# Adding x to the aggregate inside an accumulating transfer, so that PE transposes one sum

## The chip, the cores and the metric

One core of a Trainium2 chip runs the whole kernel. The metric is the time of one execution on the device in microseconds (us), median of several runs.

## What is computed

One layer of a graph network over N = 100000 nodes of width 128 and E = 50000 edges, followed by a layer norm. Everything is float32.

```python
deg = maximum(zeros(n).at[dst].add(1.0), 1.0)
edge_weight = (deg[src] * deg[dst]) ** (-0.5)
edge_msg = relu(edge_attr @ W1e + b1e) @ W2e + b2e
agg = segment_sum((x[src] + edge_msg) * edge_weight[:, None], dst)
combined = (1.0 + gin_eps) * x + agg
h = relu(combined @ W1n + b1n) @ W2n + b2n
out = (h + x) * rsqrt(mean((h + x) ** 2) + 1.2e-7) * rms_w
y = x + out
return (y - mean(y)) / sqrt(var(y) + 1e-5)
```

The change touches the line with `combined`. Since (1 + eps) x + agg = (1 + eps) (x + agg / (1 + eps)), the factor can be moved into the weights of the edges' sums and into W1n.

## The kernel before

The kernel has three stages: it counts degrees, it runs over the edges in 98 batches of 512 and scatters weighted sums of equal destinations into a scratch tensor in HBM (`agg_scratch`, the code's `agg_d`), and it runs over the nodes. Edges are sorted by destination, so that one row is written once; a last accumulating scatter (L562) adds what crosses partitions.

The node stage follows, and it is what the change touches. Node rows are laid out so that partition p holds 781 successive rows. A block is 16 of them on all 128 partitions: 8 KB a partition, 1 MB in all. There are 49 blocks (`BLOCKS`), and each is worked in four steps (`SPB`) of 4 x 128 nodes (`TB = 4`), thus 196 steps (`STEPS`). Every engine runs a hand-written software pipeline: in `node_step(n, u)` the engine does, for step number n, work on several older step indices m = n - lag, in the order in which the lines stand. Engines are tied only by semaphores.

- SP, `node_block(B)` (L488 to L503): waits until PE is done with the slot of block B-4 and loads `ag` of block B from `agg_scratch`; loads `xn` (x) of block B; then waits for `fin_ready` and `fin_last` of block B-6 (`OUT_LAG = 6`) and stores `on` to `out`. All goes through one queue, in order. `xn` and `ag` have four slots each, `on` has two.
- ACT: rms of m = n-6 (L684), cT of n-2 (L690, copies the transposed sum out of PSUM), hn of n-3 (L695), **xe of n (L701, (1 + eps) x)**, squares of n-5 (L709); once a block the spread of the layer norm (L678).
- PE: o of n-4 (L1074, L1078: bias and W2n), **the transposes of n-1 (L1087: four of xe, L1091: four of ag, accumulated into one bank)**, W1n of n-2 (L1098).
- DVE: res of n-4 (L910, h + x), bn_stats of n-8 (L927), q of n-7 (L934, times rms_w), some operations of 16 columns a block, z of n-7 (L966), and **on of the fourth column of n-18 (L975)**, which increments `fin_last`.
- POOL: xsc of n-6 (L575, four operations), which waits for ACT's rms; on of the first three columns of n-18 (L587, three operations), which increments `fin_ready`.

Two slots of `xsc` tie POOL to DVE: xsc of m waits for z of m-2, z of m waits for xsc of m. res of m has four slots, freed by q and by the squares.

Of the kernel before, what the change touches and what calls it, by code (L numbers as in the profile page):

```python
# [47 lines left out]
def build(nc, x, src, dst, edge_attr, W1n, b1n, W2n, b2n, W1e, b1e, W2e, b2e, gin_eps, rms_w, out):  # L48
# [4 lines left out]
    ALU = mybir.AluOpType  # L53
# [4 lines left out]
    E, ED = edge_attr.shape  # L58
    RMS_EPS = 1.1920929e-07
    LN_EPS = 1e-05  # L60

# [44 lines left out]
    with ExitStack() as ctx:  # L106
# [22 lines left out]
        rms_b = sb("rms_b", [P, D])  # L129
        eps1 = sb("eps1", [P, 1])  # L130
        rms_eps = sb("rms_eps", [P, 1])
        ln_eps = sb("ln_eps", [P, 1])
# [93 lines left out]
        ag = sb("ag", [P, AR, BN, D])  # L226
        xe = sb("xe", [P, 2, TB, D])
        cT = sb("cT", [P, 2, W])
# [14 lines left out]
        spread = sb("spread", [P, 2, BN])  # L243
        neg_mean = sb("neg_mean", [P, 4, BN])
        rstd = sb("rstd", [P, 4, BN])

# [15 lines left out]
        bias_ready = sem("bias_ready")  # L262
        eps_ready = sem("eps_ready")
        iota_set = sem("iota_set")
# [15 lines left out]
        lengths_ready = sem("lengths_ready")  # L280
        dd_ready = sem("dd_ready")
        lists_ready = sem("lists_ready")

# [23 lines left out]
        xn_in = sems("xn_in", XR)  # L307
        ag_in = sems("ag_in", AR)
        out_sent = sems("out_sent", 2)
        xe_ready = sem("xe_ready")  # L310
        cT_done = sem("cT_done")
# [19 lines left out]
        fin_ready = sem("fin_ready")  # L331
        fin_last = sem("fin_last")
        sp_passed = sem("sp_passed")
        pool_passed = sem("pool_passed")
# [177 lines left out]
        def _(pool):  # L512
# [52 lines left out]


            def node_step(n, u):
                m, s = n - 6, (u - 6) % 4
                if live(m, STEPS):
                    _, xsl, _, h = place(m, u - 6)  # L570
                    pool.wait_ge(rms_ready, at(m + 1))
                    need(pool, z_ready, m - 1)
                    apart(pool, pool_passed)
                    for j in range(TB):
                        last = pool.tensor_scalar(xsc[:, s % 2, j, :], xn[:, xsl, h + j, :], rms[:, s, j:j + 1], 1.0,  # L575
                                                  ALU.mult, ALU.mult)
                    last.then_inc(xsc_ready, 1)
                m, v = n - 18, (u - 18) % ZR
                if live(m, STEPS):
                    B, o, h = m // SPB, ((u - 18) // SPB) % 2, ((u - 18) % SPB) * TB  # L580
                    if h == 0:
                        pool.wait_ge(mean_ready, at(B + 1))
                        pool.wait_ge(rstd_ready, at(B + 1))
                        need(pool, out_sent[o], B // 2 * 16)
                        apart(pool, pool_passed)
                    for j in range(TB - 1):
                        last = pool.tensor_scalar(on[:, o, h + j, :], z[:, v, j, :],  # L587
                                                  neg_mean[:, v // SPB, h + j:h + j + 1],
                                                  rstd[:, v // SPB, h + j:h + j + 1], ALU.add, ALU.mult)
                    last.then_inc(fin_ready, 1)  # L590

            run(pool, STEPS, SPB * XR, node_step, tail=18, head=2)


        @block.scalar
        def _(act):
# [66 lines left out]

            act.wait_ge(dd_ready, 2)
            run(act, BATCHES, 2, edge_step, tail=1, head=2, peel=1)
# [4 lines left out]

            act.wait_ge(eps_ready, 1)

            def node_step(n, u):
# [18 lines left out]
                if live(m, STEPS):  # L692
                    act.wait_ge(hn_done, at(m + 1))
                    need(act, o_done, m - 1)
                    act.activation(hn[:, s, :], ps[2 + s][:, :], ACT.Relu, bias=b1n_c[:, 0:1]).then_inc(hn_ready, 1)  # L695
                m, s = n, u % 2
                if live(m, STEPS):
                    B, xsl, _, h = place(m, u)
                    act.wait_ge(xn_in[xsl], at(block_loads(B, XR)))
                    need(act, cT_done, m - 1)  # L700
                    act.activation(xe[:, s, :, :], xn[:, xsl, h:h + TB, :], ACT.Copy, scale=eps1[:, 0:1]  # L701
                                   ).then_inc(xe_ready, 1)
                m, v, s = n - 5, (u - 5) % ZR, (u - 5) % 4
# [8 lines left out]

            run(act, STEPS, SPB * XR, node_step, tail=18, head=2)


        @block.vector
        def _(dve):
# [120 lines left out]
            dve.wait_ge(wts_in, 16 * WEIGHTS)  # L838
            dve.tensor_scalar(eps1[:, :], eps1[:, :], 1.0, None, ALU.add).then_inc(eps_ready, 1)
            dve.wait_ge(src_cols, 2)  # L840
# [62 lines left out]
            def node_step(n, u):  # L903
                m, s = n - 4, (u - 4) % RR
                if live(m, STEPS):
                    _, xsl, _, h = place(m, u - 4)
                    dve.wait_ge(o_done, at(m + 1))
# [49 lines left out]
                if u % SPB == 1 and live(k, BLOCKS):  # L957
                    dve.wait_ge(spread_ready, at(k + 1))
                    dve.reciprocal(rstd[:, c, :], spread[:, c % 2, :]).then_inc(rstd_ready, 1)  # L959

                m, v = n - 7, (u - 7) % ZR
                if live(m, STEPS):
                    dve.wait_ge(xsc_ready, at(m + 1))
                    dve.wait_ge(q_ready, at(m + 1))
                    need(dve, fin_ready, m - ZR + 1)
                    dve.tensor_tensor(z[:, v, :, :].rearrange("p j d -> p (j d)"), ps[7][:, :],  # L966
                                      xsc[:, v % 2, :, :].rearrange("p j d -> p (j d)"), ALU.add).then_inc(z_ready, 1)
# [14 lines left out]
        def _(pe):  # L982
# [87 lines left out]
            def node_step(n, u):  # L1070
# [54 lines left out]
```

## Time and profile before

| | us |
|---|---|
| median of 3 runs | 2165.47 (2165.39 to 2170.3) |
| the profiled execution | 2150.24 |
| its span | 2148.5 |
| node stage, first ag transpose on PE to the end of the span | 1488.9 to 2148.5 |

A time in the rows is counted from the start of the span. A group's mean is its duration; successive instructions of one engine overlap in part, so an engine's pace is read from starts. "Idle before" is the engine's idle time just before an instruction, with the releaser behind the arrow. In a windows view the columns are the length, then for each engine the busy time and the number of instructions, the granted clock of PE (1.00 is 2.4 GHz), the DMA engines' busy share and GB/s.

### The profile page before, as it was taken

The page shows a single profiled execution, that of the slowest core. Times are in us where ns is not written, and L with a number is a line of the kernel's source. Part 1 is how long each engine was busy: PE and PEld are TensorE (multiplying, and loading weights), DVE is VectorE, ACT ScalarE, POOL GpSimd, SP SyncE. Part 2 cuts the span into 40 slices and gives each one's busy share as a digit, 9 for nine tenths or more (in the row PEclk, how much of TensorE's full clock was granted, in tenths as well). Part 3 has the DMA queues.
Part 4 walks back from the last instruction along what each step waited for, and adds up shares of the span by engine and source line. Part 5 has one row for each costly group of instructions (what it writes and reads, how often), then busy time and mean ns, then how long its engine had stood idle before and what let it go on. Part 6 is the DMA issues. An engine that isn't in the chain of part 4 may idle for free. (4 is left out here: it accounts for less than half of the span.)

```text
span 2148.5 us, 43403 instructions
## 1 busy us (share of the span) xinstructions
PE 1537.2 (72%) x11484; PEld 1127.5 (52%) x11484; DVE 1290.7 (60%) x4579; ACT 1118.8 (52%) x3879; POOL 1303.8 (61%) x2171
## 2 busy tenths in 40 slices
PE   1114995666666667666666677775999999999993
PEld 0002554544545445445545566664777777777772
DVE  2003996333334334343333466662999999999997
ACT  1003982222222222222222244444999999999994
POOL 5772002555555555555555545553588888888888
PEclk8556997688787886877877899997999999999997
DMA  7793001212212112111111112114366666666662
GB/s 284 302 412 144 0 3 31 53 54 53 53 53 54 53 53 54 54 53 53 53 53 53 52 56 58 59 61 183 128 252 248 234 242 248 253 253 234 235 246 115
DMA packets 83038, 275.63 MB, mean 128 GB/s; under 512 B 19110, under 2 KB 46300, under 8 KB 58396
## 3 DMA queue, kind: packets, MB, share of 16 engines
q1 hardware_dynamic: 57422, 231.16, 29.2%
q0 software_dynamic: 25136, 43.60, 6.9%
q14 instruction: 50, 0.41, 0.1%
q8 instruction: 16, 0.26, 0.1%
q10 hardware_dynamic: 414, 0.20, 0.0%
HBM read 154.37 MB, written 128.22 MB: 132 GB/s over the span
## 5 line engine op out<-in xcount | busy, mean ns | idle before, releaser
L542 POOL DMA_INDIRECT agg_scratch<-scaled,sca_i x390 | 387.6, 994 | 576.6 <-ACT scaled L661 484.2
L1022 PE MATMUL bank<-digits,picks 128*128 128x128 f16 x5488 | 441.1, 241 | 211.7 <-DVE picks L772 121.0
L1022 PEld LDWEIGHTS bank<-digits,picks 128*128 128x128 f16 x5488 | 382.6, 110 | 319.3 <-issue 165.3
L535 POOL DMA_INDIRECT xs<-in_x,src_x x391 | 377.5, 965 | 132.4 <-issue 118.8
L886 DVE TENSOR_TENSOR msg<-bank,xs 128x512 f32<-128x512 f32 x98 | 67.8, 692 | 549.7 <-issue 536.2
L575 POOL TENSOR_SCALAR xsc<-xn,rms 128x128 f32<-128x128 f32 x784 | 277.9, 370 | 128.9 <-ACT rms L684 125.5
L655 ACT ACTIVATE he<-bank,b1e_c 128x512 f32<-128x512 f32 x98 | 67.5, 689 | 512.7 <-remote 433.3
L587 POOL TENSOR_SCALAR on<-z,neg_mean,rstd 128x128 f32<-128x128 f32 x588 | 257.2, 445 | 0.0
L1000 PE MATMUL bank<-oh_hi,steps 128*128 128x512 f16 x392 | 143.6, 406 | 144.1 <-issue 125.8
L1049 PE MATMUL bank<-w2e,he 128*128 128x128 f32 x784 | 163.2, 374 | 111.9 <-ACT he L655 111.9
L1078 PEld LDWEIGHTS bank<-w2n,hn 128*128 128x128 f32 x1568 | 205.8, 191 | 70.2 <-issue 64.6
L772 DVE TENSOR_SCALAR picks<-highq,high_no 128x512 f16<-128x512 f16 x686 | 238.5, 361 | 0.0
L1098 PE MATMUL bank<-cT,w1n 128*128 128x512 f32 x392 | 220.7, 645 | 18.9 <-ACT cT L690 3.9
L709 ACT ACTIVATE squares<-res 128x128 f32<-128x128 f32 x784 | 232.4, 304 | 0.0
L759 DVE TENSOR_SCALAR oh_hi<-iota_h,dst_hi 128x782 f16<-128x782 f16 x392 | 132.8, 423 | 157.1 <-issue 100.6
L1049 PEld LDWEIGHTS bank<-w2e,he 128*128 128x128 f32 x784 | 142.1, 270 | 160.9 <-ACT he L655 159.8
L628 ACT ACTIVATE steps<-iota_h,dst_step 128x128 f16<-128x128 f16 x392 | 125.7, 392 | 163.3 <-issue 101.4
L1078 PE MATMUL bank<-w2n,hn 128*128 128x128 f32 x1568 | 206.7, 275 | 0.2 <-ACT hn L695 0.2
L641 ACT ACTIVATE eaT<-bank 64x512 f32<-64x512 f32 x98 | 58.0, 592 | 256.3 <-PE bank L1034 213.2
L927 DVE BATCH_NORM_STATS2 stats<-z 128x6 f32<-128x128 f32 x784 | 169.0, 278 | 0.0
L709 ACT ACTIVATION_READ_ACCUMULATOR squares<-res 128x1 f32 x784 | 154.4, 197 | 0.0
L864 DVE SCALAR_TENSOR_TENSOR sums<-sums,cont,bank 128x128 f32<-128x128 f32 x391 | 133.4, 341 | 33.5 <-issue 19.6
(145 smaller groups left out, 2601.2 us busy)
## 6 DMA issues: line engine op xcount, KB each, us to landing
agg_scratch<-zeros SPq DMA_DIRECT2D x48, 1024.0 KB
xn<-in_x SPq DMA_DIRECT2D x48, 1024.0 KB
ag<-agg_scratch SPq DMA_DIRECT2D x48, 1024.0 KB, 6.8
out<-on SPq DMA_DIRECT2D x48, 1024.0 KB, 4.9
highq<-src_high_scratch SPq DMA_DIRECT2D x98, 128.0 KB
ea<-in_edge_attr SPq DMA_DIRECT2D x97, 127.0 KB
xs<-in_x,src_x POOLq DMA_INDIRECT x391
agg_scratch<-scaled,sca_i POOLq DMA_INDIRECT x390
```

The costliest lines, as they stand in the source:

```text
L535: pool.indirect_dma_start(out=xs[:, b % XS, j, :], out_offset=None, in_=x, in_offset=bass.IndirectOffsetOnAxis(ap=src_x[:, t:t + 1], axis= ...
L542: pool.indirect_dma_start(out=agg_rows, out_offset=bass.IndirectOffsetOnAxis(ap=sca_i[:, t:t + 1], axis=0), in_=scaled[:, b % 2, j, :], in ...
L575: last = pool.tensor_scalar(xsc[:, s % 2, j, :], xn[:, xsl, h + j, :], rms[:, s, j:j + 1], 1.0, ALU.mult, ALU.mult)
L587: last = pool.tensor_scalar(on[:, o, h + j, :], z[:, v, j, :], neg_mean[:, v // SPB, h + j:h + j + 1], rstd[:, v // SPB, h + j:h + j + 1], ...
L709: last = act.activation(squares[:, s, j, :], res[:, s, j, :], ACT.Square, accum_out=ssq[:, v // SPB, s * TB + j:s * TB + j + 1])
L772: return dve.tensor_scalar(picks[:, s, c, :], highq[:, q, :], high_no[:, c:c + 1], None, ALU.is_equal)
L927: last = dve.bn_stats(stats[:, (v // SPB) % 2, (v % SPB) * TB + j, :], z[:, v, j, :])
L1000: pe.matmul(ps[0][:, :], steps[:, s, j, :], oh_hi[:, s, j, 0:512], start=first, stop=end)
L1022: last = pe.matmul(ps[s][:, j * P:(j + 1) * P], picks[:, s, c, j * P:(j + 1) * P], digits[:, d, c * P:(c + 1) * P], start=c + d == 0, stop ...
L1049: last = pe.matmul(ps[4 + s][:, j * P:(j + 1) * P], he[:, s, j * P:(j + 1) * P], w2e[:, :], start=False, stop=j == TB - 1)
L1078: last = pe.matmul(ps[4 + s][:, j * P:(j + 1) * P], hn[:, s, j * P:(j + 1) * P], w2n[:, :], start=False, stop=j == TB - 1)
L1098: pe.matmul(ps[2 + s][:, :], w1n[:, :], cT[:, s, :], start=True, stop=True).then_inc(hn_done, 1)
```

## The change

- POOL gets `add_block(B, a)`: wait until `ag` of block B has landed, then issue a transfer that adds x of the same block onto it in SBUF (`accum_op=add`). It stands at the head of POOL's step n = 4B - 4 (block 0 ahead of the loop, block 1 in step 0).
- PE waits for that transfer (`sum_in`) and transposes only `ag`: four transposes a step in place of eight. ACT's xe and its buffer are gone.
- eps: DVE works out 1 + eps, bounded away from zero, multiplies W1n by it and the run sums' factors `dd` and `fin_dd` by its inverse, ahead of the edge loop; ACT's edge loop waits for that (`dd_scaled`).
- on of the fourth column moves from DVE (n-18) to the end of ACT's step, at n-20, as scale times z plus `offset`; DVE works out `offset` = neg_mean * rstd once a block.

```diff
@@ gpsimd
+            def add_block(B, a):
+                if isinstance(B, int) and B == BLOCKS - 1:
+                    pool.wait_ge(ag_in[a], block_loads(B, AR))
+                    pool.dma_start(ag[:, a, 0:LASTC, :], x_main[:, B * BN:NPP, :], accum_op=ALU.add
+                                   ).then_inc(sum_in[a], 16)
+                    pool.dma_start(ag[0:NREM, a, LASTC, :], x[NPP * P:N, :], accum_op=ALU.add).then_inc(sum_in[a], 16)
+                else:
+                    pool.wait_ge(ag_in[a], at(block_loads(B, AR)))
+                    pool.dma_start(ag[:, a, :, :], x_main[:, bass.ds(at(B * BN), BN), :], accum_op=ALU.add
+                                   ).then_inc(sum_in[a], 16)
+
+            add_block(0, 0)
+
             def node_step(n, u):
+                B = n // SPB + 1
+                if u % SPB == 0 and live(B, BLOCKS):
+                    add_block(B, (u // SPB + 1) % AR)
                 m, s = n - 6, (u - 6) % 4
@@ scalar
-            act.wait_ge(dd_ready, 2)
+            act.wait_ge(dd_scaled, 1)
...
-                m, s = n, u % 2
-                if live(m, STEPS):
-                    B, xsl, _, h = place(m, u)
-                    act.wait_ge(xn_in[xsl], at(block_loads(B, XR)))
-                    need(act, cT_done, m - 1)
-                    act.activation(xe[:, s, :, :], xn[:, xsl, h:h + TB, :], ACT.Copy, scale=eps1[:, 0:1]
-                                   ).then_inc(xe_ready, 1)
...
+                m, v = n - 20, (u - 20) % ZR
+                if live(m, STEPS):
+                    B, o, h = m // SPB, ((u - 20) // SPB) % 2, ((u - 20) % SPB) * TB + TB - 1
+                    act.wait_ge(offset_ready, at(B + 1))
+                    if h < TB:
+                        need(act, out_sent[o], B // 2 * 16)
+                    act.activation(on[:, o, h, :], z[:, v, TB - 1, :], ACT.Identity, bias=offset[:, v // SPB, h:h + 1],
+                                   scale=rstd[:, v // SPB, h:h + 1]).then_inc(fin_last, 1)
@@ vector
-            dve.tensor_scalar(eps1[:, :], eps1[:, :], 1.0, None, ALU.add).then_inc(eps_ready, 1)
+            link(dve.tensor_scalar(eps1[:, :], eps1[:, :], 1.0, None, ALU.add))
+            dve.tensor_scalar(eps_sign[:, :], eps1[:, :], 0.0, 2.0, ALU.is_ge, ALU.mult)
+            link(dve.scalar_tensor_tensor(eps_abs[:, :], eps1[:, :], -1.0, eps1[:, :], ALU.mult, ALU.max))
+            link(dve.tensor_scalar(eps_abs[:, :], eps_abs[:, :], EPS_FLOOR, None, ALU.max))
+            link(dve.scalar_tensor_tensor(eps1[:, :], eps_sign[:, :], -1.0, eps_abs[:, :], ALU.add, ALU.mult))
+            dve.tensor_scalar(w1n[:, :], w1n[:, :], eps1[:, 0:1], None, ALU.mult)
+            link(dve.reciprocal(eps_inv[:, :], eps1[:, :]))
+            dve.wait_ge(dd_ready, 2)
+            dve.tensor_scalar(dd[:, :], dd[:, :], eps_inv[:, 0:1], None, ALU.mult)
+            dve.tensor_scalar(fin_dd[:, :], fin_dd[:, :], eps_inv[:, 0:1], None, ALU.mult).then_inc(dd_scaled, 1)
...
+                k, c = (n - 18) // SPB, ((u - 18) // SPB) % 4
+                if u % SPB == 2 and live(k, BLOCKS):
+                    dve.wait_ge(rstd_ready, at(k + 1))
+                    dve.tensor_tensor(offset[:, c, :], neg_mean[:, c, :], rstd[:, c, :], ALU.mult
+                                      ).then_inc(offset_ready, 1)
...
-                m, v = n - 18, (u - 18) % ZR
-                if live(m, STEPS):
-                    B, o, h = m // SPB, ((u - 18) // SPB) % 2, ((u - 18) % SPB) * TB + TB - 1
-                    dve.wait_ge(rstd_ready, at(B + 1))
-                    if h < TB:
-                        need(dve, out_sent[o], B // 2 * 16)
-                    dve.tensor_scalar(on[:, o, h, :], z[:, v, TB - 1, :], neg_mean[:, v // SPB, h:h + 1],
-                                      rstd[:, v // SPB, h:h + 1], ALU.add, ALU.mult).then_inc(fin_last, 1)
@@ tensor
-                    pe.wait_ge(xe_ready, at(m + 1))
+                    pe.wait_ge(sum_in[asl], at(block_loads(B, AR)))
                     need(pe, cT_ready, m - 1)
                     for j in range(TB):
-                        pe.matmul(ps[s][:, j * P:(j + 1) * P], xe[:, s, j, :], ident[:, :], is_transpose=True,
-                                  start=j == 0, stop=False)
-                    pe.wait_ge(ag_in[asl], at(block_loads(B, AR)))
-                    for j in range(TB):
                         last = pe.matmul(ps[s][:, j * P:(j + 1) * P], ag[:, asl, h + j, :], ident[:, :],
-                                         is_transpose=True, start=False, stop=j == TB - 1)
+                                         is_transpose=True, start=j == 0, stop=j == TB - 1)
```

## Rows read from the trace of the kernel before

**Rows 1.** The page: busy digits of 40 slices of the span, two engines.

```profile
ACT  1003982222222222222222244444999999999994
POOL 5772002555555555555555545553588888888888
```

**Rows 2.** Windows: the steady part of the node stage.

```profile
1552.40:2103.70 551.30, 533.93 (x3268) 390.49 (x3267) 537.88 (x1720) 544.75 (x2108) 467.65 (x1204) 1.00 0.64 241
```

**Rows 3.** Timeline of POOL, steps 21 and 193: start, us, instructions.

```profile
1549.46 1.41 POOL L575 TENSOR_SCALAR xsc<-xn,rms 128x128 f32<-128x128 f32 x4 [0.46 <-ACT rms L684]
1550.85 1.30 POOL L587 TENSOR_SCALAR on<-z,neg_mean,rstd 128x128 f32<-128x128 f32 x3
...
2101.04 1.41 POOL L575 TENSOR_SCALAR xsc<-xn,rms 128x128 f32<-128x128 f32 x4 [0.43 <-ACT rms L684]
```

**Rows 4.** Timeline of all engines, ACT's and one POOL row shown.

```profile
1802.37 0.29 ACT L684 ACTIVATE rms<-ssq,rms_eps 128x4 f32<-128x4 f32 x1
...
1802.89 1.45 POOL L575 TENSOR_SCALAR xsc<-xn,rms 128x128 f32<-128x128 f32 x4 [0.51 <-ACT rms L684]
...
1803.61 0.72 ACT L701 ACTIVATE xe<-xn,eps 128x512 f32<-128x512 f32 x1
...
1804.22 0.31 ACT L709 ACTIVATE squares<-res 128x128 f32<-128x128 f32 x1
```

**Rows 5.** Timeline of DVE, one step.

```profile
1805.04 0.69 DVE L966 TENSOR_TENSOR z<-bank,xsc 128x512 f32<-128x512 f32 x1 [0.19 <-DVE bank L934]
1805.65 0.34 DVE L975 TENSOR_SCALAR on<-z,neg_mean,rstd 128x128 f32<-128x128 f32 x1
1805.90 0.68 DVE L910 TENSOR_TENSOR res<-bank,xn 128x512 f32<-128x512 f32 x1
```

**Rows 6.** Timeline of PE, an early step: four transposes of each.

```profile
1496.71 0.60 PE L1087 MATMUL bank<-ident,xe 128*128 128x128 f32 x4
1497.14 0.60 PE L1091 MATMUL bank<-ident,ag 128*128 128x128 f32 x4
```

**Rows 7.** Timeline of SP's queue.

```profile
1552.43 0.34 SPq L503 DMA_DIRECT2D out<-on  x1
...
1783.55 0.36 SPq L503 DMA_DIRECT2D out<-on  x1
1784.16 0.33 SPq L481 DMA_DIRECT2D ag<-agg_scratch  x1
```

**Rows 8.** Waits of SP's queue, then ag's time to landing, both 1700 to 2000.

```profile
SPq L349 <- DVE on L975: 238.3, 23, 10.6
...
DMA to landing us min/median/max: 6.3/6.8/7.1
```

**Rows 9.** Timeline of POOL: scatters, and the one that accumulates.

```profile
1477.41 0.98 POOL L542 DMA_INDIRECT agg_scratch<-scaled,sca_i  x1 [0.30 <-issue]
1480.48 1.60 POOL L562 DMA_INDIRECT agg_scratch<-scaled,fin_i  x1 [2.09 <-issue]
```

**Rows 10.** DMA queues: 1700 to 2000, then 1481 to 1484: packets, MB, share.

```profile
q1 hardware_dynamic: 10112, 73.54, 64.7%
...
q0 software_dynamic: 144, 0.07, 26.4%
```

**Rows 11.** Timeline of PE: the start of the node stage.

```profile
1488.88 1.12 PE L1091 MATMUL bank<-ident,ag 128*128 128x128 f32 x4 [10.61 <-DMA ag<-agg_scratch]
```

**Rows 12.** Windows: the DMA engines at the start of the node stage.

```profile
1482.50:1483.00 0.50, 0.00 (x0) 0.00 (x0) 0.00 (x0) 0.00 (x0) 0.00 (x0) 0.50 0.82 43
...
1492.00:1496.00 4.00, 4.00 (x15) 2.43 (x14) 0.00 (x0) 2.43 (x5) 0.00 (x0) 0.68 0.86 360
```

**Rows 13.** Waits, 335 to 349: the first batch of edges.

```profile
DVE msg L886 <- PE bank L1049: 4.6, 1, 4.6
```

**Rows 14.** Timeline of POOL: the tail.

```profile
2104.22 1.41 POOL L575 TENSOR_SCALAR xsc<-xn,rms 128x128 f32<-128x128 f32 x4 [0.48 <-ACT rms L684]
...
2127.23 17.23 POOL L587 TENSOR_SCALAR on<-z,neg_mean,rstd 128x128 f32<-128x128 f32 x39
```

More of the change, by code:

```diff
@@ L59, in build @@
     RMS_EPS = 1.1920929e-07
+    EPS_FLOOR = 1e-12
     LN_EPS = 1e-05
@@ L130, in build @@
         eps1 = sb("eps1", [P, 1])
+        eps_abs = sb("eps_abs", [P, 1])
+        eps_sign = sb("eps_sign", [P, 1])
+        eps_inv = sb("eps_inv", [P, 1])
         rms_eps = sb("rms_eps", [P, 1])
@@ L226, in build @@
         ag = sb("ag", [P, AR, BN, D])
-        xe = sb("xe", [P, 2, TB, D])
         cT = sb("cT", [P, 2, W])
@@ L244, in build @@
         neg_mean = sb("neg_mean", [P, 4, BN])
+        offset = sb("offset", [P, 4, BN])
         rstd = sb("rstd", [P, 4, BN])
@@ L262, in build @@
         bias_ready = sem("bias_ready")
-        eps_ready = sem("eps_ready")
         iota_set = sem("iota_set")
@@ L281, in build @@
         dd_ready = sem("dd_ready")
+        dd_scaled = sem("dd_scaled")
         lists_ready = sem("lists_ready")
@@ L308, in build @@
         ag_in = sems("ag_in", AR)
+        sum_in = sems("sum_in", AR)
         out_sent = sems("out_sent", 2)
-        xe_ready = sem("xe_ready")
         cT_done = sem("cT_done")
@@ L332, in build @@
         fin_last = sem("fin_last")
+        offset_ready = sem("offset_ready")
         sp_passed = sem("sp_passed")
@@ L590, in node_step @@
                     last.then_inc(fin_ready, 1)
-            run(pool, STEPS, SPB * XR, node_step, tail=18, head=2)
+            run(pool, STEPS, SPB * XR, node_step, tail=18, head=2, peel=1)
         @block.scalar
@@ L668, in _ @@
                            ).then_inc(fin_scaled, 1)
-            act.wait_ge(eps_ready, 1)
             def node_step(n, u):
@@ L711, in node_step @@
                     last.then_inc(ssq_ready, 1)
-            run(act, STEPS, SPB * XR, node_step, tail=18, head=2)
+                m, v = n - 20, (u - 20) % ZR
[6 more added lines that the diff above has]
+                                   scale=rstd[:, v // SPB, h:h + 1]).then_inc(fin_last, 1)
+            run(act, STEPS, SPB * XR, node_step, tail=20, head=2)
         @block.vector
@@ L905, in node_step @@
                 if live(m, STEPS):
-                    _, xsl, _, h = place(m, u - 4)
+                    B, xsl, _, h = place(m, u - 4)
+                    dve.wait_ge(xn_in[xsl], at(block_loads(B, XR)))
                     dve.wait_ge(o_done, at(m + 1))
@@ L958, in node_step @@
                     dve.wait_ge(spread_ready, at(k + 1))
+                    need(dve, fin_last, (k - 3) * SPB)
                     dve.reciprocal(rstd[:, c, :], spread[:, c % 2, :]).then_inc(rstd_ready, 1)
+                k, c = (n - 18) // SPB, ((u - 18) // SPB) % 4
[3 more added lines that the diff above has]
+                                      ).then_inc(offset_ready, 1)
                 m, v = n - 7, (u - 7) % ZR
@@ L965, in node_step @@
                     need(dve, fin_ready, m - ZR + 1)
+                    need(dve, fin_last, m - ZR + 1)
                     dve.tensor_tensor(z[:, v, :, :].rearrange("p j d -> p (j d)"), ps[7][:, :],
                                       xsc[:, v % 2, :, :].rearrange("p j d -> p (j d)"), ALU.add).then_inc(z_ready, 1)
-                m, v = n - 18, (u - 18) % ZR
-                if live(m, STEPS):
-                    B, o, h = m // SPB, ((u - 18) // SPB) % 2, ((u - 18) % SPB) * TB + TB - 1
-                    dve.wait_ge(rstd_ready, at(B + 1))
-                    if h < TB:
-                        need(dve, out_sent[o], B // 2 * 16)
-                    dve.tensor_scalar(on[:, o, h, :], z[:, v, TB - 1, :], neg_mean[:, v // SPB, h:h + 1],
-                                      rstd[:, v // SPB, h:h + 1], ALU.add, ALU.mult).then_inc(fin_last, 1)
             run(dve, STEPS, SPB * XR, node_step, tail=18, head=2)
```

## The prediction

> **What bounds the kernel now.** I read the busy line and the slices first. The last 28% of the span is one stage, the node loop of 196 steps, where ACT shows nines and POOL eights; nothing before it uses what the change touches, but for a few tiny DVE operations [rows 1]. The window over the steady part says the same: of 551.3 us PE is busy 533.9, DVE 537.9, ACT 544.8, POOL 467.7, the DMA engines 0.64, with TensorE granted its upper level of 2.4 GHz throughout [rows 2]. So I asked for every engine's own pace in the timeline, by starts and not by durations, since neighbours overlap. One `POOL` step (four xsc, three on) starts at 1549.46 in step 21 and at 2101.04 in step 193: 172 steps in 551.6 us, 3.207 a step, 12.83 a block of four steps, 43 blocks [rows 3].
>
> ACT is busy 98.8% [rows 2]; of its step's 3.2 us, start to start, xe is 0.61 and a square of 128x128 lasts 0.31 [rows 4]. DVE is busy 97.6%, of which on (L975) is 0.25 a step [rows 2, 5]. Neither has slack. POOL has 1.41 + 1.30 = 2.71 of work, then about 0.5 of waiting for ACT's rms [rows 3]. PE is busy 96.8% by a view in which overlapping matmuls count whole; four xe transposes are 0.43 of a step [rows 6]. So ACT and DVE bound the stage together, POOL is hidden by 0.5 us a step.
>
> The third thing to read is SP. Each block it issues out, then ag, then xn, within about 1 us, after having waited for L975, 238.3 us in 23 blocks [rows 7, 8]. ag lands 6.3 to 7.1 us after its issue, 6.8 in the median [rows 8]. Nobody waits for it today, because PE wants it eight steps later. That distance is what the change spends.
>
> **Part by part. Removed:** xe leaves ACT (0.61 a step); four transposes leave PE (0.43); on of the fourth column leaves DVE (0.25) and costs ACT one 128x128 activation, about 0.30 like a square. ACT: 3.2 - 0.61 + 0.3 = 2.9 a step at most. PE: under 2.8. DVE: 12.83 - 4 x 0.25 = 11.8 a block; the new offset is one operation of 16 columns a block and goes where DVE waits 0.19 between q and z [rows 4 to 6]. If that were all, the block would be limited by POOL: 4 x 2.71 = 10.85 plus the issue of the transfer, 12.35 with the 1.5 below.
>
> **Added: the issue on POOL.** No direct transfer is issued by POOL in this trace. The nearest rows are its indirect ones: 0.98 for a plain scatter, with 0.30 of issue gap after it, and 1.60 for the one that accumulates [rows 9]; from below, SP's issue of a 1 MB transfer, 0.33 [rows 7]. I take 1.5 (nearest to the accumulating row), bounds 0.33 and 1.9.
>
> **Added: the wait, and where it stands.** This decides the case. Steps are numbered n as in the code. add_block(B) stands at the head of POOL's step n = 4B-4 and waits for ag_in of block B. SP issues ag B only after the out of block B-7, and that waits for on of step index m = 4B-25: on POOL at n = m+18 = 4B-7, and now on ACT at n = m+20 = 4B-5. So POOL reaches its wait only two steps (5.4 us) after it released SP itself, and about when ACT's on is done, and everything queued behind the wait on POOL stands: xsc and on. DVE's z waits for xsc, res stands behind z, ACT's squares wait for res, and ACT's own on behind them. Before, slot and order were the same, but only PE waited, in step 4B+1.
>
> This is a loop, and it can be added up. From the end of POOL's step 4B-7: to SP's issue of out 0.28, to the issue of ag 0.61, landing 6.8, waking POOL 0.2 (as from the end of rms to xsc, 1802.66 to 1802.89), the add's issue 1.5, then POOL's steps 4B-4 and 4B-3, which end with the on that releases the next block: 2 x 2.71 = 5.42. Sum **14.8 us a block** [rows 3, 4, 7, 8, 9]. The other branch of the loop is shorter: from the add's issue xsc 1.41, wake 0.15, z to res 0.61 (as z to on now), res 0.68, wake 0.15, four squares of 0.31, on 0.3, some 4.5 against 5.42, so POOL's own order is the last thing. Every other engine needs less than 14.8 a block, so it sets the pace: 14.8 - 12.83 = +1.97, times 43 = **+85 us**. With landing 6.3 and issue 0.33 the block is 13.1 (+12 us), with 7.1 and 1.9 it is 15.5 (+115).
>
> **Added: the transfer.** Three transfers keep 16 engines busy for 0.647 x 300 us in 23 blocks, thus 8.4 a block, 2.8 per MB [rows 10]. The accumulating one reads two sources. The only accumulate in the trace (128 rows of 512 B) occupies 26.4% of 3 us, 0.79 us for 0.07 MB, 11 us per MB [rows 10]. So the bounds are 2.8 and 11; I take twice the plain time, 5.6, since it reads ag and x where a load reads one of them, and rows of 8 KB should shed most of what each packet costs. Then the data moves from about 10 to 15.6 us after the release (first bytes 2 us after the issue, as at L562: issue 1480.48, bytes from 1482.5 [rows 9, 12]), is there before PE's step 4B+1 at about 16.8, and hardly meets the next out.
> The Trainium skill (Collectives: The Full Stack, § The bandwidth ceiling) says that a reduce in the DMA engines is half as fast as a copy because it reads two sources. This trace has no 8 KB accumulate to confirm it. By that rule the transfer would be an estimated 5.6 us too, and the sum would not change; the rule speaks against the change only in that a load of 1 MB is bought at the price of two.
>
> **Start.** PE's first ag transpose starts at 1488.88, 10.6 us after it was ready, with four ag loads in flight [rows 11]. Now it waits also for the add: issue 1.5 to bytes 2.1, transfer 5.6 shared with the other ag loads, which by the windows keep the engines busy until about 1495.4, 4.4 us from there [rows 12], landing 0.5: +8.2 to +12.6, taken **+10.6**. **Steps 0 to 21** have all loads ahead and run at DVE's pace: 15 x 0.25 and a little for the first six on PE: **-6**. **Edge stage:** eight small linked DVE operations and the scaling of dd stand ahead of ACT's first batch, some 2 us in all; DVE waits 4.6 us for PE in that batch [rows 13] and hides most of it: 0 to 2, taken **+1**. **Tail:** without ag, POOL goes at 2.71 instead of 3.09 for the 7 steps up to its last xsc (2104.22 to 2125.8), then its 39 on take 17.2 us as now [rows 14]: **-2.5**.
>
> Sum: 85 + 10.6 - 6 + 1 - 2.5 = +88. Against the profiled execution (2148.5 and 1.7 around it, 2150.2) this is 2238. The median of the runs shown is 15.2 higher, so I put the same +88 on it: 2165.5 + 88 = **2253**.
>
> **Rivals.** (a) Faster: the wait never binds, because ag has landed when POOL asks. POOL is then the bound with 10.85 + 1.5 = 12.35 a block (DVE 11.8): -0.48 x 43 = -21, with the other terms -18, so 2148. For it: ag nowhere shows up as waited for in the steady part. Against it: the order of SP's queue, and 23 waits of 10 us there [rows 8]. It decides if release to landing falls from 7.9 to 5.9 us or less. (b) Same time: a cheap issue (0.33) and a landing under 6.3; 13.1 a block or a bit less, 2165 to 2182. (c) The transfer binds: at 8 to 11 us for the add, the DMA engines need 16.4 to 19.4 a block, above 14.8. It decides from 6.4 us. At 10 us: 18.4, +240 and the start: 2410. For it: the only accumulate row. Against it: that row's packets of 512 B. (d) The relief of ACT and PE as such brings nothing, since DVE loses only 0.25 a step; this holds in all cases and is in the sums.
>
> **Chances.** 14.8 a block with its bounds 0.67 (own range 2185 to 2290); (c) 0.14; (a) 0.12; (b) 0.07. A measurement of this kernel can tell about 0.3% (6.5 us) from no change: faster 0.12, same 0.06, slower 0.82. The range takes the whole of the first case, the upper part of (b) and the lower part of (c), which leaves out (a) and the upper (c), 0.2: 2175 to 2335.
>
> **What would show it.** Right: SP's out, ag, xn come every 14.8 us instead of 12.83, and its wait ends on POOL's L587 twin; the add's issue stands in POOL's timeline after some 2.5 us idle each block, "idle before <- DMA ag"; PE, DVE and ACT fall to 80% busy together; DMA share rises to about 0.95 in the steady part. Landing of ag stays 6.8 (7.5 or more: the adds collide with out). Wrong: blocks under 12.83 us and no idle time before the add (a); PE waiting for the add itself, with blocks above 16 (c); an issue far from 1.5 us shifts every block by the difference, 43 times.

## The result, and the profile after

The changed kernel takes 2258.9 us (median of 4 runs, 2254.53 to 2259.56); before, with the same number of runs, 2165.43 (2165.34 to 2170.3). The ratio is 1.043, 95% interval 1.0416 to 1.0443: 93.5 us slower, forecast 2253. The profiled execution took 2258.38 us, its span is 2256.7.

The page's slices of the changed kernel, ACT, POOL, PE's granted clock, each digit a fortieth of the span, against [rows 1]:

```profile
ACT  1005952222222222222222444428777778777785
POOL 5771004555555555555555445536677877778778
PEclk8557988776887777877778999969888888889986
```

Windows over the whole steady part and over a piece of it (length, then busy us and instructions of PE, PE's weight loads, DVE, ACT and POOL, granted clock, DMA share, GB/s), against [rows 2]:

```profile
1578.00:2180.00 602.00, 468.50 (x2402) 334.42 (x2442) 503.39 (x1503) 473.14 (x1992) 462.25 (x1165) 0.89 0.94 283
1700.00:1950.00 250.00, 195.54 (x1003) 139.94 (x1020) 212.52 (x629) 197.23 (x833) 194.93 (x492) 0.89 0.95 284
```

ACT's nines of [rows 1] are sevens and eights. PE is busy 78%, DVE 84%, ACT 79%, POOL 77% where three of them stood at 97 to 99%: no engine is a bound any more, and DMA traffic rose from 241 to 283 GB/s. When all engines fall together, the pace is set either by something that goes round between them or by the DMA engines, whose share is 0.94. The timelines show that something goes round; which of the two it is, e2 below decides. POOL, start, us, instructions, idle time before in brackets, against [rows 3]:

```profile
1794.54 0.86 POOL L580 DMA_DIRECT2D ag<-in_x  x1 [3.36 <-DMA ag<-agg_scratch]
1795.13 1.68 POOL L596 TENSOR_SCALAR xsc<-xn,rms 128x128 f32<-128x128 f32 x4
1796.53 1.51 POOL L608 TENSOR_SCALAR on<-z,neg_mean,rstd 128x128 f32<-128x128 f32 x3
1797.82 1.56 POOL L596 TENSOR_SCALAR xsc<-xn,rms 128x128 f32<-128x128 f32 x4
1799.22 1.39 POOL L608 TENSOR_SCALAR on<-z,neg_mean,rstd 128x128 f32<-128x128 f32 x3
...
1809.18 0.88 POOL L580 DMA_DIRECT2D ag<-in_x  x1 [3.15 <-DMA ag<-agg_scratch]
```

and SP's queue between these two adds, against [rows 7]:

```profile
1800.79 0.36 SPq L508 DMA_DIRECT2D out<-on  x1
1801.40 0.33 SPq L486 DMA_DIRECT2D ag<-agg_scratch  x1
1801.83 1.22 SPq L486 DMA_DIRECT2D xn<-in_x  x1
...
1815.49 0.36 SPq L508 DMA_DIRECT2D out<-on  x1
```

POOL's on of 1799.22 ends at 1800.61 and releases out at 1800.79. ag is issued at 1801.40, POOL meanwhile works two more steps and then stands idle for 3.15 us, which the trace puts down to that very ag. The add starts at 1809.18, two steps follow, and out is issued at 1815.49. The loop of the forecast is there, one round in 14.7 us.

What is waited for from 1700 to 2000 in all engines, then in SP's queue (us in total, times, longest), and the median time to landing of three transfers, against [rows 8]:

```profile
POOL ag L580 <- DMA ag<-agg_scratch: 64.5, 20, 4.2
DVE z L1005 <- POOL xsc L596: 21.5, 16, 2.7
```

```profile
SPq L354 <- ACT on L732: 235.3, 20, 13.3
SPq L508 <- POOL on L608: 8.1, 15, 0.6
```

```profile
out<-on SPq DMA_DIRECT2D x20, 1024.0 KB, 4.8
ag<-agg_scratch SPq DMA_DIRECT2D x20, 1024.0 KB, 6.8
...
ag<-in_x POOLq DMA_DIRECT2D x20, 1024.0 KB, 8.0
```

POOL waits for ag in each of the 20 blocks, 3.2 us on average. DVE's z shows the wait handed on: xsc comes late. SP waits long for ACT's on and then, in 15 of the 20 rounds, another 0.5 us for POOL's: both branches of the loop end nearly together, and POOL's is mostly the last (in the round shown ACT's on ended at 1814.92, POOL's at 1815.32). In the other 5 ACT's on came last.

The DMA queues in the same stretch (packets, MB, share of 16 engines), against [rows 10]:

```profile
q1 hardware_dynamic: 8919, 64.94, 56.5%
q0 software_dynamic: 2880, 20.97, 38.4%
```

q1 holds SP's plain transfers, q0 POOL's accumulating ones. 0.565 x 300 / 64.94 = 2.61 us of 16 engines per 10^6 bytes plain, 0.384 x 300 / 20.97 = 5.49 accumulating; for a block of 1024 KB that is 2.74 and 5.76. These shares count the time that packets took, and the packets of two queues can be under way at once, so they needn't add up to a limit of 1.0.

The start and the tail, against [rows 11, 14]:

```profile
1505.62 0.98 POOL L580 DMA_DIRECT2D ag<-in_x  x1 [7.06 <-DMA ag<-agg_scratch]
...
1518.01 1.97 PE L1118 MATMUL bank<-ident,ag 128*128 128x128 f32 x8 [25.44 <-DMA ag<-in_x]
...
1571.23 1.44 POOL L596 TENSOR_SCALAR xsc<-xn,rms 128x128 f32<-128x128 f32 x4
...
2209.67 1.50 POOL L596 TENSOR_SCALAR xsc<-xn,rms 128x128 f32<-128x128 f32 x4
...
2234.22 16.88 POOL L608 TENSOR_SCALAR on<-z,neg_mean,rstd 128x128 f32<-128x128 f32 x39
```

The rows of 1571.23 and 2209.67 are POOL's steps 21 and 193, between which the forecast counts its 43 blocks. The two traces can be cut at the same events, from the end of the edge stage (the start of the last accumulating scatter) to the end of the span:

| us | before | after | difference | forecast |
|---|---|---|---|---|
| scatter to first transpose | 1480.48 to 1488.88 | 1496.96 to 1518.01 | +12.65 | +10.6 |
| to POOL's step 21 | 60.58 | 53.22 | -7.4 | -6 |
| to POOL's step 193, 43 blocks | 551.58 (12.83 each) | 638.44 (14.85 each) | +86.9 | +85 |
| to the end of the span | 47.46 | 47.03 | -0.4 | -2.5 |
| sum | 668.0 | 759.7 | +91.7 | +87 |

The scatter itself stands 16.5 us later after than before. The profiled execution of before was 15.2 us below its own median, and in e9, the same kernel profiled again, the scatter stands at 1493.92. So most of the 16.5 is a difference between executions.

By SP's issues instead of POOL's steps, the 42 distances from the first out of the loop to the last take 538.95 us before and 623.27 after: 12.83 and 14.84 us.

### The profile page after: what moved, and what is told of

It reads as the page before. It is cut to its first block and busy times, and to the rows that moved or that the text cites. A ratio compares the mean times of both kernels' runs of the same rounds, so it can differ in the third digit from the quotient of the medians.

```text
span 2256.7 us, 41743 instructions
## 1 busy us (share of the span) xinstructions
PE 1471.6 (65%) x10554; PEld 1083.9 (48%) x10700; DVE 1284.0 (57%) x4440; ACT 1067.3 (47%) x3879; POOL 1335.6 (59%) x2221
## 5 line engine op out<-in xcount | busy, mean ns | idle before, releaser
L1053 PE MATMUL bank<-digits,picks 128*128 128x128 f16 x5488 | 452.0, 241 | 275.3 <-issue 144.4
L1125 PE MATMUL bank<-cT,w1n 128*128 128x512 f32 x392 | 239.4, 696 | 141.8 <-ACT cT L710 136.6
L596 POOL TENSOR_SCALAR xsc<-xn,rms 128x128 f32<-128x128 f32 x784 | 301.2, 501 | 32.2 <-ACT rms L704 16.5
L608 POOL TENSOR_SCALAR on<-z,neg_mean,rstd 128x128 f32<-128x128 f32 x588 | 276.1, 542 | 0.0
L1109 PEld LDWEIGHTS bank<-w2n,hn 128*128 128x128 f32 x1568 | 230.9, 212 | 80.2 <-issue 72.1
L1080 PE MATMUL bank<-w2e,he 128*128 128x128 f32 x784 | 169.1, 383 | 113.2 <-ACT he L676 111.2
L1109 PE MATMUL bank<-w2n,hn 128*128 128x128 f32 x1568 | 229.7, 295 | 7.3 <-DVE res L942 4.4
L1080 PEld LDWEIGHTS bank<-w2e,he 128*128 128x128 f32 x784 | 147.1, 279 | 99.9 <-ACT he L676 99.6
L1005 DVE TENSOR_TENSOR z<-bank,xsc 128x512 f32<-128x512 f32 x196 | 134.6, 687 | 87.1 <-POOL xsc L596 56.3
L942 DVE TENSOR_TENSOR res<-bank,xn 128x512 f32<-128x512 f32 x196 | 133.7, 682 | 57.7 <-PE bank L1109 56.9
```

What stands on the lines that cost most here:

```text
L1053: last = pe.matmul(ps[s][:, j * P:(j + 1) * P], picks[:, s, c, j * P:(j + 1) * P], digits[:, d, c * P:(c + 1) * P], start=c + d == 0, stop ...
L1080: last = pe.matmul(ps[4 + s][:, j * P:(j + 1) * P], he[:, s, j * P:(j + 1) * P], w2e[:, :], start=False, stop=j == TB - 1)
L1109: last = pe.matmul(ps[4 + s][:, j * P:(j + 1) * P], hn[:, s, j * P:(j + 1) * P], w2n[:, :], start=False, stop=j == TB - 1)
L1125: pe.matmul(ps[2 + s][:, :], w1n[:, :], cT[:, s, :], start=True, stop=True).then_inc(hn_done, 1)
```

## Experiments

In all tables and sentences, a block is the mean distance of SP's out issues in the loop. The experiments ran on several chips, on which the kernel before takes one of two times: 2169 us for e1 to e4, e9 and e10, and 1779 to 1784 us for the others. The node stage is the same on both (from the first load of ag to the end 663.1 us in e9, 665.8 us in e11); what is shorter lies ahead of it. So differences in us are compared, each against the kernel before on its own chip.

### e1_plain: the same wait and transfer, but the transfer doesn't accumulate

The transfer copies x over ag, so the aggregate is left out of what the kernel computes. The last block's two transfers have the same edit.

```diff
-                    pool.dma_start(ag[:, a, :, :], x_main[:, bass.ds(at(B * BN), BN), :], accum_op=ALU.add
+                    pool.dma_start(ag[:, a, :, :], x_main[:, bass.ds(at(B * BN), BN), :]
...
```

> The changed kernel with the transfer on POOL copying x over ag instead of adding it (the aggregate is left out of the result): same size, same place, same waits. Theory A (the loop from POOL's on through SP's queue, ag's landing and POOL's wait sets the block): the transfer is not in the loop, so a block stays 14.3 to 14.7 us; only the start gets shorter, by 3 to 7 us; 2240 to 2255 us in all. Theory B (the DMA engines, busy 0.94, are the bound): their work falls from about 14.2 to 11.3 us a block and the block to 12.3 or less; 2140 to 2160 us.

2232.17 us (2 runs), 63 us above before: ratio 1.0297 (1.0235 to 1.0359). A block takes 14.24 us. Its queues, 1700 to 1950, and its wait:

```profile
q1 hardware_dynamic: 7522, 54.81, 58.2%
q0 software_dynamic: 2497, 18.10, 21.1%
```

```profile
POOL ag L580 <- DMA ag<-agg_scratch: 48.9, 17, 3.5
```

A plain transfer from POOL costs 0.211 x 250 / 18.10 = 2.91 us per 10^6 bytes, 3.06 a block, against 5.76 with the addition, and the DMA engines have a fifth of their time free. The block hardly cares: 14.24 us is just under the 14.3 to 14.7 that were expected of the loop, and 2232 just under 2240. The loop is nearly all there without the accumulation, whose price in it is 0.6 us a block.

### e2_lag7 and e3_lag7_plain: ag is released a block earlier

```diff
-    OUT_LAG = 6
+    OUT_LAG = 7
```

SP now issues ag of block B after the out of block B-8, so POOL's wait is six steps away from its release in place of two. e3 has the diff of e1 too, and so computes without the aggregate.

> The changed kernel with OUT_LAG 7 instead of 6: SP queues ag and xn of a block four steps earlier, nothing else moves. Theory A alone: POOL no longer waits for ag, the block falls to POOL's or DVE's own pace, 11.8 to 12.3 us, about 2140 us. Theory A with B close behind it: the block stops at the DMA engines' 3 x 2.83 + 5.76 = 14.2 us, about 2235 us, with the DMA share at 1.0. Theory B alone: no change, 2258.

> Both: OUT_LAG 7 and the transfer as a plain copy (the aggregate is left out of the result). Neither the loop nor the DMA engines (11.3 us) bind; the block is DVE's 11.8 or POOL's 4 x 2.69 + 0.6 = 11.4, so 11.8 to 12.1; about 2130 us. If the block stays above 13 us there is a third limit that neither theory has.

e2: 2155.16 us (3 runs), ratio 0.9931 (0.9909 to 0.9954), 14 us below before, a block 12.40. e3: 2143.9 (2 runs), ratio 0.989 (0.9854 to 0.9926), a block 12.30. e2's window, its queues and its wait, 1700 to 1950:

```profile
1700.00:1950.00 250.00, 216.74 (x1202) 150.22 (x1220) 240.09 (x752) 233.22 (x996) 234.12 (x589) 0.99 1.02 338
```

```profile
q1 hardware_dynamic: 8714, 63.39, 61.3%
q0 software_dynamic: 2909, 21.21, 40.8%
```

```profile
POOL ag L580 <- DMA ag<-agg_scratch: 5.5, 7, 0.9
```

Both blocks are a little longer than was expected (11.8 to 12.3 and 11.8 to 12.1 us).

This is the experiment that decides. All the work and all the transfers of the change are there, and one number of the order of SP's queue takes 2.4 us off each block: POOL's wait falls from 64.5 us in 20 blocks to 5.5 us in as many. So the bytes of the transfer and its issue didn't set the pace by themselves; they cost what they add to the loop. A theory that I had added on the way fell with it: that the queues' shares add up to a floor of some 14 us a block (0.95 of 14.8). Here the same four megabytes move in 12.4 us at 338 GB/s and a share of 1.02. What the DMA engines' load does show is in the landings: ag 11.9 us, the add 12.8 (6.8 and 8.0 after), and they are early enough for that. The price of a transfer moves with the load as well: from e2's lines it is 0.408 x 250 / 21.21 = 4.81 us per 10^6 bytes accumulating, 5.04 a block, and 2.5 a block plain.

### e4_relief and e7_direct: the relief without the wait and the transfer

e4 takes the transfer and the wait out of the changed kernel and leaves x out of the sum. e7 keeps the sum whole: PE transposes xn as it was loaded, then ag, into one bank. The diff shows e7's part on PE.

```diff
...
-                    pe.wait_ge(sum_in[asl], at(block_loads(B, AR)))
+                    pe.wait_ge(xn_in[xsl], at(block_loads(B, XR)))
                     need(pe, cT_ready, m - 1)
                     for j in range(TB):
+                        pe.matmul(ps[s][:, j * P:(j + 1) * P], xn[:, xsl, h + j, :], ident[:, :], is_transpose=True,
+                                  start=j == 0, stop=False)
+                    pe.wait_ge(ag_in[asl], at(block_loads(B, AR)))
+                    for j in range(TB):
                         last = pe.matmul(ps[s][:, j * P:(j + 1) * P], ag[:, asl, h + j, :], ident[:, :],
-                                         is_transpose=True, start=j == 0, stop=j == TB - 1)
+                                         is_transpose=True, start=False, stop=j == TB - 1)
...
```

> The changed kernel without the transfer and its wait (x is left out of what W1 is applied to): only what the change takes off PE, ACT and DVE. Both theories: DVE's pace, 11.8 us a block, no delay at the start; 2165 - 43 x 1.0 - 8 = about 2114 us. If DVE's operation that was taken away cost nothing, it would stay at 12.8 and about 2160.

> The changed kernel without the transfer; PE transposes x straight out of xn and ag after it, accumulated in one bank, as before but with no copy by ACT (eps stays folded into W1 and the run sums). PE gets its 0.43 us a step back and stays under DVE's pace: 12.0 to 12.1 us a block as in the run without x, no delay at the start: 2118 to 2126 us, faster than both kernels. If PE were the limit after all, 2135 or more.

e4: 2119.73 us (2 runs), ratio 0.9779 (0.975 to 0.9807), -49.4 us. e7: 1737.46 (4 runs), ratio 0.9741 (0.9725 to 0.9758), -46.3 us. Windows of e4 and e7:

```profile
1700.00:1950.00 250.00, 219.52 (x1224) 151.91 (x1244) 239.87 (x767) 237.39 (x1014) 225.52 (x581) 1.00 0.68 260
```

```profile
1300.00:1600.00 300.00, 289.28 (x1895) 224.27 (x1893) 287.98 (x921) 285.53 (x1221) 270.44 (x696) 1.00 0.69 260
```

Both have blocks of 12.08 us (11.8 was expected of e4, 12.0 to 12.1 of e7), whatever PE does: four more transposes a step raise PE from 88% to 96% busy and move nothing. DVE and ACT are at 96 and 95%. DVE lost 0.25 us a step, 1.0 a block, and the block lost 0.75 (12.83 to 12.08). In a block DVE's busy time went from 12.52 us (97.6% of 12.83) to 11.59 (95.9% of 12.08), -0.93, and its idle time from 0.31 to 0.49. e7 computes the same as both kernels and is faster than either: 46 us below before, where the changed kernel is 83 to 94 above. The sum of ag and x costs no time in PE's bank here, as PE has room for it; the price of the changed kernel is that it was moved elsewhere.

### e8_fold_only: only xe is taken away

The kernel before with eps folded and PE transposing xn and ag; on of the fourth column stays on DVE. DVE's res gets a wait for xn, which ACT's xe had covered before.

> The kernel before with eps folded and xe gone, PE transposing xn and ag, but on of the fourth column left on DVE. If DVE bounds the stage as well as ACT, taking 0.61 us a step off ACT alone gives little: 12.75 to 12.83 us a block, 2158 to 2164 us. If ACT was the one bound and DVE only followed it: 12.1 or less, about 2125.

1781.82 us (10 runs), ratio 0.999 (0.998 to 1.0001), -1.9 us. Window of e8, and of the kernel before on another chip of the same level (e11), 1300 to 1600:

```profile
1300.00:1600.00 300.00, 268.22 (x1750) 207.54 (x1751) 295.34 (x926) 237.69 (x1040) 253.58 (x647) 1.00 0.64 243
```

```profile
1300.00:1600.00 300.00, 286.90 (x1732) 211.17 (x1768) 295.60 (x933) 295.26 (x1140) 251.76 (x652) 1.00 0.65 245
```

ACT falls from 98% to 79% busy, DVE stays at 98.5%, and a block takes 12.99 us against 12.90 (12.75 to 12.83 was expected). Of the two engines that bound this stage together, relieving ACT alone is worth nothing. e8 and e7 ran on the same chip and differ on ACT and DVE in the fourth column's on alone, 12.99 against 12.08 us: the 46 us of e7 hang on the one small operation that left DVE, 0.91 us a block, and on ACT having room for it.

### e5_wait_only, e9_before_again, e11_before_beside, e12_wait_beside: the wait alone

```diff
             def node_step(n, u):
+                B = n // SPB + 1
+                if u % SPB == 0 and live(B, BLOCKS):
+                    pool.wait_ge(ag_in[(u // SPB + 1) % AR], at(block_loads(B, AR)))
...
```

This is the kernel before, with nothing added but the wait at the head of POOL's step 4B-4.

> The kernel before with nothing of the change but the wait: POOL waits for ag of block B at the head of its step 4B-4, as add_block does, and issues nothing. Theory A: the loop closes on the wait alone: on of POOL to out 0.28, to ag 0.61, landing 6.8, waking POOL 0.2 to 0.4, two steps of POOL 5.42 = 13.3 to 13.5 us a block against 12.83: 2185 to 2195 us. Rival: what costs in the change is the transfer and its issue, a wait alone is absorbed by the slack of POOL (0.5 us a step): 2165.

1795.75 us (4 runs), ratio 1.0062 (1.0046 to 1.0079): +12.0 us, with blocks of 13.3 us as expected, but short of the expected 20 to 30 us in all. Three more runs asked where the rest was.

> The kernel before, unchanged. It asks what a block of it takes where the wait alone (13.3 us a block) and the folded eps (13.0 us a block) were measured, since the profile of before (12.83 us a block) was taken elsewhere. If the wait alone was dear in the loop but cheap in total (+12.0 us instead of the 20 that 43 blocks at +0.47 us give) because a block of before is itself longer there, its blocks here take 13.0 to 13.1 us. If the missing 8 us lie outside the loop, they take 12.8 to 12.9 us.

> The kernel before, unchanged, as a profile on the same chip for the next run. A block takes 12.8 us.

> The wait alone once more: it cost 12.0 us in all, where its blocks (13.3 us, 12.8 before) said 20. From its own profile the node stage was 17 us longer than before's. If the rest was a difference between executions ahead of the node stage, the whole costs 15 to 20 us here and the two profiles differ by that in the node stage alone. If the wait really costs 12, the two node stages differ by 12, and a block of the kernel beside it takes 13.0 us.

e9 (2167.44 us, ratio 0.9994, 0.9981 to 1.0007) ran where the kernel before takes 2169 us and gave 12.81 us, which says nothing of the chips where it takes 1780. e11 (1779.93, ratio 1.0005, 0.9996 to 1.0015) and e12 (1793.14, ratio 1.0081, 1.0065 to 1.0098) ran side by side: +14.2 us, just under the expected 15 to 20. Blocks are 12.90 and 13.31, so 41 blocks give +16.8. The end gives 1.9 back, where the last blocks have no such wait any more: from the first out to POOL's last 39 on it is 577.3 and 592.1 us, +14.9. Part of the missing 8 us was thus a block of before that is 0.07 longer on that chip (3 us in 43 blocks), part the end; the rest stands ahead of the node stage and isn't explained. The node stage from the first load of ag is 665.8 and 681.7 us, +15.9. POOL's timeline in e12, then its wait, 1300 to 1600:

```profile
1371.06 1.41 POOL L578 TENSOR_SCALAR xsc<-xn,rms 128x128 f32<-128x128 f32 x4 [2.42 <-DMA ag<-agg_scratch]
1372.45 1.34 POOL L590 TENSOR_SCALAR on<-z,neg_mean,rstd 128x128 f32<-128x128 f32 x3
```

```profile
POOL xsc L578 <- DMA ag<-agg_scratch: 52.6, 22, 2.8
```

The wait leaves POOL idle for 2.4 us, 22 times in 300 us, once a block, and lengthens a block by only 0.41. POOL had 0.5 us a step of slack [rows 3], 2.0 a block, and the wait eats that first.

### e6_late_add: the add stands two steps later in POOL's order

```diff
-                B = n // SPB + 1
-                if u % SPB == 0 and live(B, BLOCKS):
+                B = (n - 2) // SPB + 1
+                if u % SPB == 2 and live(B, BLOCKS):
```

> The changed kernel with add_block two steps later in POOL's own order (head of step 4B-2), SP as it was. Theory A: the next release of SP (POOL's on in step 4B-3) now stands ahead of the wait, the loop spans two blocks and stops binding; 12.3 to 12.6 us a block as with OUT_LAG 7, about 2155 us. Rival: the transfer then lands too late for PE's step 4B+1 (8 to 13 us after its issue, three steps being 9 us) and PE takes the wait over: above 13 us, 2190 us or more.

1824.97 us (2 runs), ratio 1.0228 (1.0207 to 1.0248), +41.2 us, a block 13.66. Its waits, 1300 to 1600:

```profile
POOL ag L580 <- DMA ag<-agg_scratch: 39.0, 21, 2.5
PEld bank L1118 <- DMA ag<-in_x: 29.1, 17, 3.4
PE bank L1118 <- DMA ag<-in_x: 25.8, 15, 3.2
```

POOL's wait shrinks only to 1.9 us a block and PE, which never waited for the add in the changed kernel's steady part, now waits for it. The rival was right here. The loads land later too, ag 9.2 us after its issue in place of 6.8, so that POOL still waits. Between ag's landing and PE's use there was room for one of two things, a transfer of 8 us or two steps of POOL; moving the add alone by two steps didn't mend it.

### e10_after_again: the changed kernel, repeated

> The changed kernel, unchanged. The wait's loop (POOL's output, the next load behind it on SP, its landing, the add's issue, POOL's two steps) and its transfers have nothing to do with the edge stage: a block takes 14.7 to 14.9 us again, and the kernel is 88 to 98 us longer than before. If the price hung on the clock that was granted to TensorE in the edge stage, or on how far the edge stage's end was from the node stage's start, it would be another: below 80 or above 105 us.

2252.87 us (2 runs), ratio 1.0388 (1.0318 to 1.0459), +83.1 us, a block 14.55. Both are a little under what was expected (88 to 98 us, 14.7 to 14.9). Two terms of the loop, next section, are a little shorter, the landing of ag above all; I can't say why.

## Why the prediction was right

**The loop.** Mean over 39 rounds of the profiled execution, and of the runs that take one part away (us; the sums are the blocks):

| term | forecast | after | after again | e1, plain copy |
|---|---|---|---|---|
| SP: out issued to ag issued | 0.61 | 0.66 | 0.66 | 0.66 |
| ag issued to the add's start (landing, wake) | 6.8 + 0.2 | 7.68 | 7.54 | 7.34 |
| add's start to xsc's start | 1.5 | 0.60 | 0.60 | 0.59 |
| two steps of POOL and SP's wake | 5.42 + 0.28 | 5.85 | 5.76 | 5.64 |
| sum | 14.8 | 14.79 | 14.56 | 14.23 |

The mechanism, the loop and its turning through SP's queue, is shown. That its sum is right to 0.1 us is luck in part: terms missed in opposite directions. The issue that I took from the accumulating scatter [rows 9] is 0.60 us from start to start, in the lower half of my bounds (0.33 to 1.9): a direct transfer is no indirect one, and SP's 0.33 was the better neighbour. That is 0.9 too much in the forecast. In return, three terms were longer. From ag's landing to the add's start it is 0.62 us, where I had the 0.2 of one engine's wake. ag itself lands after 7.06 us in the mean of these rounds in place of 6.8 (6.71 before, 6.68 in e1, 6.92 in e10). The two steps and SP's wake took 0.15 more. Together with SP's 0.05 this gives the 0.9 back. What stands in the 0.62 us can be read in part, from the sequencer's records of the add's line, 1700 to 2000:

```profile
L580 POOLq MOVE ag<-in_x x20: 29/29/38, 1705.1 to 1984.7; - x20
L580 POOL DMA_DIRECT2D ag<-in_x x20: 857/866/883, 1705.6 to 1985.2; - x20
```

A register instruction of that line, which stands behind the wait, begins 0.54 us before the add and lasts 0.03. In the kernel with the wait alone POOL goes on with xsc 0.30 us after the landing. So issuing a transfer behind the wait costs some 0.3 us ahead of its start and 0.6 behind it. What fills the half microsecond between the register instruction and the start the trace doesn't say.

The other branch was forecast 0.9 us shorter than POOL's. It is 0.4 shorter in the round shown, and in 10 of the loop's 43 outs ACT's on ended last. ACT's on takes 0.49 us, not 0.3, which is 0.2 of the difference. The forecast that POOL's own order is always the last thing was too strong: SP's wait showed up on both names.

e12 checks the same sum without the add: 0.28 + 0.61 + 6.8 + 0.2 + 5.42 = 13.3, measured 13.31 in the kernel that has the wait alone. Then come 0.9 us for the issue and what stands ahead of it (e1, 14.24), and 0.6 for the accumulation (14.84), for which the loop's sum had no term. Of it 0.34 us lie ahead of the add's start, and that is ag's landing, 7.06 against e1's 6.68; 0.21 lie in the last term. The xsc behind the accumulating transfer lasts 1.68 us, in e1 1.41, but that is not a slower pace of POOL: from each of its four groups to the next, start to start, it is 1.42, 1.29 and 1.40 us, in e1 1.41, 1.28 and 1.39. What reaches the loop is the end of the on that releases SP, which lasts 1.44 us against 1.30; the rest of the 0.21 I can't place. Why operations last longer behind an accumulating transfer isn't shown. With the relief alone a block is 12.08 (e4, e7), so wait, issue and accumulation together cost 2.76 a block.

**The transfer.** Forecast 5.6 us of 16 engines, measured 5.76 (5.04 in e2), from bounds of 2.8 and 11. The factor of two was right. The rule of the Trainium skill (Collectives: The Full Stack, § The bandwidth ceiling), half a copy's speed for a reduce, is borne out in size: 5.76 against 2.74 for SP's plain transfers is a factor of 2.1, against POOL's plain one in e1, 3.06, it is 1.9. That two sources are the reason no run here shows. Rival (c) would have needed 6.4. That the floor is not where the added shares reach 1.0 is shown by e2; how much more the engines could carry isn't.

**Start and first steps.** The two terms were mis-sized against each other. The start is +12.65, at the upper bound (12.6) and not at 10.6: the first add took 12.3 us to land, the next two 14.9 and 16.6, while four ag loads were in flight. Steps 0 to 21 gave -7.4 instead of -6. POOL ended step 21 at 1573.95, but the first out went only at 1578.71, since it is released by ACT's on, which stands two steps later in its order. The 43 blocks' +86.9 against +85 hides two misses more. That delay put some 4 us into them. And the last add stands at the head of step 188, so the 43rd block, steps 189 to 193, had no wait in it and took 10.8 us, not 14.8.

**Tail and edge stage.** The tail gave -0.4 against -2.5. POOL went at 2.90 us a step there, not at 2.71 (its last xsc starts at 2232.80, its step 194 at 2212.49), and 5.6 us pass from the end of its last on to the end of the span, where it was 4.0 before. The edge term (+1) can't be told from execution to execution; e8, which has all of it, is 1.9 us faster than before.

**Rivals.** (a), the wait that never binds, would have been true with one change of a constant: e2 releases ag six steps ahead and reaches 12.40 (forecast for (a): 12.35), though 2155 and not 2148. That the two blocks agree is luck. With the issue's measured 0.60 us, POOL's own pace would be 10.85 + 0.6 = 11.45, and what holds e2 at 12.40 and e3 at 12.30 wasn't separated. Its condition, 5.9 us from release to landing, is where the loop falls to 12.83; for 12.35 it would have been 5.4. (b), with the cheapest issue and landing, had no term for what stands ahead of the issue nor for the price of accumulating in the loop; only the wait-only kernel comes near its 13.1 a block. (c) fell. (d) held in that xe's removal alone is worth nothing (e8); with DVE's on it is 0.75 to 0.91 a block (e4 against 12.83, e7 against 12.90 and against e8), where the forecast had 1.0.

**Signs.** Out, ag and xn every 14.84 us: yes. 2.5 us of idle time before each add: 3.2 us. PE, DVE and ACT at 80% together: 78, 84, 79. DMA share 0.95: 0.94 to 0.95. Landing of ag 6.8: the median from 1700 to 2000 is 6.8, but single ones take up to 7.9 and the mean is 7.06 against 6.71 before, so the transfers do get a little in each other's way. What the list had not: TensorE's granted clock, which was 1.00 in the steady part before, is 0.89 in it after and 0.99 in e2, where the waits are gone. It fell where PE had begun to wait 20% of the time. None of the loop's terms is work of PE; what the clock adds to a block all the same I didn't separate.

## What to carry to other kernels

When a wait moves to another engine, find what releases it and count how many of that engine's own steps lie between its release and its wait: if a load's issue, landing and the work in between don't fit, the whole pipeline turns at that loop's pace, and every engine's busy share falls together. A sum of such terms that comes out right proves the loop only with runs that take one term away. Before counting on a relief, look for the second engine at the same height; here 0.6 us a step off ACT was worth nothing, and 0.25 us off DVE together with it 46 us. A sum that TensorE makes by accumulating two transposes in one bank cost no transfer and no wait on POOL here, and releasing the load one block earlier gave 2.4 of the loop's 2.76 us back.

## What the runs showed of the hardware

- A direct transfer of 1 MB issued by POOL cost it 0.6 us from start to start, accumulating or not. Behind a wait it started 0.62 us after the landing waited for, where an xsc started 0.30 us after it (e12). Where POOL didn't have to wait (e2, e3), the transfer started without a gap behind the on before it.
- Accumulating x onto 1 MB in SBUF took 5.76 us of 16 DMA engines' time, plain 2.74 from SP and 3.06 from POOL (e1), and landed 8.0 us after its issue against 5.2 (e1). With the transfers crowded together (e2) it landed after 12.8 and took 5.04.
- POOL's four xsc operations lasted 1.68 us in place of 1.41 just behind the issue of an accumulating transfer, and not behind a plain one. The starts of what followed were not later for it.
- A DMA share of 0.95 was not a limit: with the order mended, the same transfers went at 338 GB/s, share 1.02.
- The edge stage took some 384 us less on some chips than on others (first load of ag at 1112.80 in e11, 1497.23 in e9), with the node stage the same within 3 us. The windows of the same kernel in its edge stage show TensorE's granted clock at 0.92 (e11) and 0.77 (e9) of 2.4 GHz. Whether the clock is the whole of it wasn't tried.

```profile
400.00:1000.00 600.00, 409.06 (x4304) 331.55 (x4363) 323.91 (x1363) 228.72 (x681) 433.65 (x441) 0.92 0.23 67
```

```profile
400.00:1200.00 800.00, 506.43 (x4168) 397.01 (x4228) 316.47 (x1312) 220.64 (x655) 466.92 (x475) 0.77 0.18 53
```
